# Feed-forward part of a transformer layer on one core: batch 1's rows loaded first, gathers three tiles ahead, and VectorE's closing work in another order

## The reference

```python
h = _layernorm(x) * (1 + ca) + sa
x = x + ga * attn(h, wq, wkv_a, wkv_b, wo)
h = _layernorm(x) * (1 + cb) + sb
# ffn(h): the expert is w2(gelu(h @ g + gb) * (h @ w1 + b1)) + b2
aff = sigmoid(h @ wa); p, i = top_k(aff, 2); p = p / sum(p)
ffn = h + sum over the 2 shared experts + sum over the 2 chosen experts of p * expert(h)
x = x + gb * ffn
```

## Time and profile before

| | us |
|---|---|
| median of 3 runs | 1361.8 |
| lowest and highest | 1360.68, 1362.64 |
| the profiled execution's own time | 1362.64 |
| its span, first to last instruction | 1360.8 |
| TensorE busy | 1321.8 (97%) |
| VectorE busy | 850.3 (62%) |
| ScalarE busy | 687.1 (50%) |
| POOL busy | 384.3 (28%) |

### The profile page before, as it was taken

The page is one execution under the profiler, slowest core; times in us unless marked ns, Lnnn a source line. Parts: engine busy times, 40 slices in busy tenths (PEclk is TensorE's granted clock), DMA queues, the critical chain, the costliest instruction groups (busy, mean ns, idle before and its releaser), DMA issues. The chain is left out here.

```text
span 1360.8 us, 22755 instructions
## 1 busy us (share of the span) xinstructions
PE 1321.8 (97%) x6836; PEld 1102.7 (81%) x6836; DVE 850.3 (62%) x1753; ACT 687.1 (50%) x1615; POOL 384.3 (28%) x353
## 2 busy tenths in 40 slices
PE   6899999999999999999999999997999999999997
PEld 3667777888888888888888888886887888888886
DVE  5788755666666666666666777666666444344568
ACT  3334427666666666666666776663312323232232
POOL 0336465000013092030550302800032232323164
PEclk9999999999999999999999999999999999999999
DMA  9999989967677769696687899793646999894375
GB/s 290 382 343 375 369 299 319 341 223 237 205 276 272 237 231 327 206 341 207 226 301 268 289 316 329 278 354 146 246 156 244 336 347 363 289 368 172 128 235 171
DMA packets 160057, 375.57 MB, mean 276 GB/s; under 512 B 23164, under 2 KB 80576, under 8 KB 147696
## 3 DMA queue, kind: packets, MB, share of 16 engines
q1 hardware_dynamic: 144416, 314.32, 66.0%
q0 software_dynamic: 15568, 60.32, 12.5%
HBM read 245.84 MB, written 128.22 MB: 275 GB/s over the span
## 5 line engine op out<-in xcount | busy, mean ns | idle before, releaser
L1193 ACT ACTIVATE a_pr<-a_pr,a_stat 128x128 f32<-128x128 f32 (+3 forms) x256 | 141.9, 555 | 71.4 <-DVE a_stat L1272 71.4
L1212 ACT ACTIVATE a_pT<-x_banks 128x512 fp32r<-128x512 f32 (+1 forms) x192 | 87.1, 531 | 75.6 <-PE x_banks L1415 75.6
L1199 ACT ACTIVATE a_pr<-a_pr,a_stat 128x128 f32<-128x128 f32 (+3 forms) x256 | 122.3, 550 | 0.5 <-DVE a_stat L1277 0.5
L1399 PE MATMUL x_banks<-a_pT,a_cv 128*128 128x512 f32 (+1 forms) x576 | 120.5, 354 | 0.3 <-issue 0.3
L1399 PEld LDWEIGHTS x_banks<-a_pT,a_cv 128*128 128x128 f32 x576 | 103.4, 188 | 21.2 <-issue 0.7
L1272 DVE CUSTOM_DVE_ANT_0 a_pr<-a_psS,f_mask 128x256 f32<-128x256 f32 (+2 forms) x192 | 101.2, 555 | 23.7 <-PE a_psS L1387 23.3
L1300 DVE TENSOR_TENSOR a_pT<-x_banks,a_pT 128x512 fp32r<-128x512 f32 (+1 forms) x192 | 103.4, 594 | 12.6 <-ACT a_pT L1212 12.6
L101 PE MATMUL x_banks<-a_hT,a_wqk 128*128 (+1 forms) x256 | 99.9, 390 | 1.0 <-DVEq L1259 1.0
L102 PE MATMUL x_banks<-a_hT,a_wqk 128*128 (+1 forms) x256 | 99.7, 390 | 0.0
L103 PE MATMUL x_banks<-a_hT,a_wqk 128*128 (+1 forms) x256 | 99.6, 389 | 0.0
L1288 DVE SCALAR_TENSOR_TENSOR a_qT<-x_banks,a_qT 128x512 fp32r<-128x512 f32 x64 | 44.3, 692 | 85.6 <-ACT a_qT L1203 85.6
(11 more groups left out here) (378 smaller groups left out, 3611.9 us busy)
## 6 DMA issues: line engine op xcount, KB each, us to landing
w1s_d<-a_ws SPq DMA_DIRECT2D x72, 512.0 KB, 3.5
a_wqk<-wqk_d SPq DMA_DIRECT2D x64, 512.0 KB, 5.0
a_mh<-mhl_d SPq DMA_DIRECT2D x32, 1024.0 KB, 5.9
s_ring<-w1s_d SPq DMA_DIRECT2D x16, 2048.0 KB, 10.0
w2s_d<-a_ws SPq DMA_DIRECT2D x72, 256.0 KB, 3.9
qpe_d<-p_qs SPq DMA_DIRECT2D x16, 1024.0 KB, 5.1
a_rw<-in_L_ffn_rw SPq DMA_DIRECT2D x128, 128.0 KB, 3.5
a_qpe<-qpe_d SPq DMA_DIRECT2D x64, 256.0 KB, 2.7
```

The costliest lines, as they stand in the source:

```text
L1193: nc.scalar.activation(pr[i], pr[i], ACT.Exp, bias=nmax[:, i:i + 1], scale=-1.0, accum_out=rsum[:, i:i + 1]).then_inc(ex, 1)
L1199: nc.scalar.activation(pr[i], pr[i], ACT.Copy, scale=rinv[:, i:i + 1]).then_inc(nr, 1)
L1212: nc.scalar.activation(pT[:, u, 0, dst], src, ACT.Copy).then_inc(p_hi, 1)
L1399: last = nc.tensor.matmul(two_of(bank)[:, :, (2 - k) * P:2 * P], cv[:, j, cs], pT[:, :, ps, o:o + k * P], start=m == 0, stop=m == len(part ...
```

## The change

Three edits.

1. In SP's list `rows(1, 1)` stands ahead of the three small transfers on `wa_in`.
2. `AHEAD` is 3: gathers are issued when the tile three before has landed. (SP's wait for `turns[AHEAD - 1]` is written `turns[1]`, the same as before.)
3. VectorE's and ScalarE's lists at the end are rewritten. Tile 2 is taken after slice 2 of batch 3 rather than slice 3. In batch 2 ScalarE scales two to three tiles more ahead of the gelus. VectorE does `weighted` of tiles 9 to 13 ahead of time; tiles 12 and 13 and 15 no longer use `finish` but three new functions: `gated` (the sum times the gate row), `based` (plus the residual) and `joined` (the product from `final` times the gate row into `ys`, and that added). So of these tiles the multiplication and the residual do not need the products.

```diff
-        AHEAD = 2
+        AHEAD = 3
-        tiles_m = {LAST: [[], [0], [1], [2, 3, 4, 5, 6, 7, 8]], 2: [[9], [10], [11], []]}
+        tiles_m = [[], [0], [1, 2], [3, 4, 5, 6, 7, 8]]
...
+                rows(1, 1)
                 sp.dma_start(waf[:, :, :], K.ins["L0_ffn_wa"].rearrange("(c p) e -> p c e", p=P)).then_inc(wa_in, 16)
                 sp.dma_start(bst[0:SH], K.ins["L0_ffn_sgb"]).then_inc(wa_in, 16)
                 sp.dma_start(bst[SH:2 * SH], K.ins["L0_ffn_sb1"]).then_inc(wa_in, 16)
-                rows(1, 1)
                 rows(2, 0)
...
-                for m in range(NU):
+                scaled(9)
+                scaled(10)
+                for m, i in enumerate((11, 13, 14, 15)):
                     gelu(2, m)
+                    scaled(i)
                     y_high(2, m)
-                    if m < NU - 1:
-                        scaled(9 + m)
-                for i in range(12, 16):
-                    scaled(i)
+                    if m == 0:
+                        scaled(12)
...
+                def gated(i):
+                    dve.wait_ge(cch, done[0])
+                    tt_(at[:, i % NA], at[:, i % NA], gb4[:, turns[i] // TB], ALU.mult).then_inc(cch, 1)
+                    done[0] += 1
+                def based(i):
+                    b, t = turns[i] // TB, turns[i] % TB
+                    dve.wait_ge(cch, done[0])
+                    dve.wait_ge(s_in[b], 16)
+                    tt_(at[:, i % NA], at[:, i % NA], total[b][:, t], ALU.add).then_inc(cch, 1)
+                    done[0] += 1
+                def joined(i):
+                    n, b, t = done[0], turns[i] // TB, turns[i] % TB
+                    dve.wait_ge(sh_o, place_of[b] * TB + t + 1)
+                    if i == NT - 1:
+                        dve.wait_ge(o_ok, i - 1)
+                    tt_(ys[:, i % 2], final[b][t], gb4[:, b], ALU.mult).then_inc(cch, 1)
+                    dve.wait_ge(cch, n + 1)
+                    tt_(at[:, i % NA], at[:, i % NA], ys[:, i % 2], ALU.add).then_inc(o_ok, 1)
+                    done[0] = n + 1
...
-                for m in range(NU):
-                    times(2, m)
-                    y_low(2, m)
-                    if m < NU - 1:
-                        whole(9 + m)
-                for i in (12, 13, 14):
-                    weighted(i)
-                finish(12)
-                finish(13)
+                weighted(9)
+                weighted(10)
+                times(2, 0)
+                weighted(11)
+                y_low(2, 0)
+                finish(9)
+                weighted(12)
+                times(2, 1)
+                gated(12)
+                y_low(2, 1)
+                finish(10)
+                weighted(13)
+                times(2, 2)
+                based(12)
+                y_low(2, 2)
+                finish(11)
+                gated(13)
+                times(2, 3)
+                based(13)
+                y_low(2, 3)
+                weighted(14)
                 weighted(15)
+                gated(15)
+                joined(12)
+                based(15)
+                joined(13)
                 finish(14)
-                finish(15)
+                joined(15)
```

More of the change, by code:

```diff
@@ L1742, in _ @@
                     sp.wait_ge(y_out[v], 16 * ((NBLK - v + 1) // 2))
-                sp.wait_ge(r_in[turns[AHEAD - 1]], 32)
+                sp.wait_ge(r_in[turns[1]], 32)
                 sp.dma_start(total[2][:, :, :], K.base_d[2].rearrange("t p n -> p t n")).then_inc(s_in[2], 16)
@@ L1904, in _ @@
                     y_high(LAST, m)
-                    for i in tiles_m[LAST][m]:
+                    for i in tiles_m[m]:
                         scaled(i)
-                for m in range(NU):
+                scaled(9)
+                scaled(10)
+                for m, i in enumerate((11, 13, 14, 15)):
                     gelu(2, m)
+                    scaled(i)
                     y_high(2, m)
-                    if m < NU - 1:
-                        scaled(9 + m)
-                for i in range(12, 16):
-                    scaled(i)
+                    if m == 0:
+                        scaled(12)
             @block.vector
```

## The result

The changed kernel takes 1358.34 us (median of 12 runs, 1357.48 to 1359.76) against 1360.95 for the kernel before on the same chip (12 runs, 1358.53 to 1363.16): ratio 0.9979, 95% interval 0.9970 to 0.9988, a gain of 2.6 us. I forecast 1359.7 and a gain of 2.1. The profiled execution of the changed kernel took 1359.19 us, its span 1357.4.

The account below looks back on a forecast made before the run. TensorE is busy 97% of the span, so gains lie in the first transfer, the gathers' pace and VectorE's list. Front 0.4 plus end 1.7 gave 2.1 us off the 1361.8 median: 1359.7, range 1356.9 to 1362.9 for 8 in 10.

Parts of the forecast that it names:

- likeliest case: Whole kernel: gain of 1 to 3.2 us, around 1359.7, own range 1358.6 to 1360.8; chance 0.42.
- front's gain: Start of the feed-forward part: issuing batch 1's rows earlier gains 0.4 us, between 1.1 gained and 1.2 lost.
- W: Front: time at which the small transfers on `wa_in` are complete, put at 948.5, ends 945 and 950.
- VectorE's side: Front: VectorE, waiting for the small transfers, can start the second `times` at W + 14.7, 963.2; TensorE allows 962.8.
- TensorE's transposes 0.8 to 1.1 us sooner: Front, sign of edit 1: batch 1's transposes start that much sooner after the barrier.
- L2035's counterpart 3 to 4 us later: Front, sign of edit 1: VectorE's operation on the router's weights, behind `wa_in`, starts that much later.
- The gathers: POOL from tile 4 on: three in flight give 2.75 us a tile instead of 3.50, plus 1.1 for stalls.
- Rival C: Gathers: third tile in flight brings no pace, DMA engines set it; 3.9 later at the end, 1365.3; chance 0.12.
- The lists: End: 13 operations instead of 16 behind the last `y_low`, 9.3 us; VectorE ends at S + 20.1, 1.7 us gained.
- S: End: time at which ScalarE can scale tile 13, put at 1336.5, ends 1332.7 and 1342.1.
- A: End: gathers come sooner, S at 1334.7 or before, tail's floor gives 3.5; gain 3.9 to 4.6, 1357.6; chance 0.26.
- B: Gain cancels: front loses up to 1.2 through `wa_in`, or S lies near 1338.2; 1361.5; chance 0.20.

Follow-up runs that it names:

- small_last: The changed kernel with the three small transfers behind both batches' rows: 1363.11 us, ratio 1.0012 to the kernel before.
- changed_again: The changed kernel measured once more, unaltered, beside other kernels on one chip: 1358.34 us, ratio 0.9983 to the kernel before.
- tail_only: The changed kernel with batch 1's rows back behind the small transfers (edits 2 and 3 without 1): 1359.35 us, ratio 0.9993 to the kernel before.
- tail_again: Edits 2 and 3 without edit 1, the same kernel timed in another job: 1357.1 us, ratio 0.9978 to the kernel before.
- lists_only: The changed kernel with AHEAD = 2 and the small transfers first (edit 3 alone): 1363.85 us, ratio 1.0030 to the kernel before.
- no_lists: The kernel before with edits 1 and 2, ScalarE's and VectorE's lists as before: 1359.32 us, ratio 0.9988.
- ahead3_only: The kernel before with AHEAD = 3 alone (edit 2), lists as before: 1358.37 us, ratio 0.9986.
- small_on_pool: The changed kernel with the three small transfers issued by POOL at the block's start: 1362.04 us, ratio 1.0006 to the kernel before.

## Why the prediction held, step by step

The forecast was 1359.7, the result 1358.34, inside the range of 1356.9 to 1362.9 and 0.3 below the likeliest case's own edge of 1358.6. Of the 1.4 us by which the time came below the forecast, 0.85 are the baseline (1361.8 from three runs, 1360.95 from twelve) and 0.5 the gain. The range is no strong test: the kernel before, at 1360.95, lies in it too. What can be tested are the parts. The mechanism at the end held, with one size off; the front's gain did not show. That a front taken 0.4 too well and an end taken 0.3 to 1.4 too low partly cancel is luck.

**W and VectorE's side.** Predicted: W 6.6 us after SP's first issue, `times` at W + 14.7. Measured: 5.7, and 963.77 - 949.43 = 14.3. `wa_in` does hold VectorE, as predicted. "TensorE's transposes 0.8 to 1.1 us sooner" and "L2035's counterpart 3 to 4 us later" came as about 1.3 sooner (950.03 - 943.87 = 6.2 after the part's start, before 7.5) and 2.8 later (5.86 after it against 3.05). Both lie just outside what I had named, and the second `times`, 1.5 us sooner in the profiled pair, does too. Off by 0.9 was W, since the rows landed in 5.4 us and not in 6.44. I had carried over a duration, and it goes with the place in SP's list: 6.3 to 6.5 us in the five traces with the small transfers ahead of the rows, 5.2 to 5.5 in the nine with the rows first, in small_last too, where the second 1 MB follows right behind. Why is open.

**The front's gain, 0.4.** This step is not borne out. Timed alone edit 1 has 1.0007 (0.9998, 1.0016), which leaves room for a gain of 0.3 us at most; with edit 2 beside it it has 0.9988 against 0.9986 without it, and with edits 2 and 3 0.9979 and 0.9983 against 0.9993 and 0.9978. But what I subtracted from was unsound: the 21.39 us of before hold 6.8 us at the lower clock, and I wrote that the clock didn't matter since VectorE's side has no product in it. That is so after the edit; before it TensorE's side decided. By the traces, what edit 1 does is to trade a front of 19.1 to 21.4 for one of 19.9.

**The gathers.** Predicted 2.75 a tile and 1.1 of stalls over nine tiles, 2.87 together; measured 2.83. Tile 15 was issued at 1334.36, ahead of the 1337 that I had named. Rival C rested on a DMA share of 0.95 with two tiles in flight; over 1306 to 1322 us the share rose from 0.85 to 0.93, and the pace came all the same: a share near 1 did not show a bound. The term that I mis-sized is the way from a tile's first issue to ScalarE's use: 6.0 taken, 1334.27 - 1329.33 = 4.94 measured, below my lowest row (5.6). That put `scaled(13)` at 41.0 us after the first gather, not at 42.6, and so at 1334.27 and not at 1336 to 1337, and the last `y_low` at 1345.46 and not at 1347 to 1348. Single gathers of the changed kernel took this long from issue to landing, over 1303 to 1340 us:

```profile
DMA to landing us min/median/max: 3.6/4.7/7.0
```

With the second gather 1.26 us behind the first, a tile takes 4.9 us at the least and 6.0 at the median; my 6.0 was the median, and tile 13 had the least, in changed_again too (40.43 - 35.50 = 4.9).

**The lists.** Last `y_low` to VectorE's end: 9.3 predicted, 9.38 measured. `scaled(13)` to VectorE's end: 20.1 predicted, 1354.84 - 1334.27 = 20.6 measured. S sooner by 1.6 and 0.5 more behind it give 1.1 more than my 1.7, 2.8: the end won 2.7 us in the profiled pair, 3.1 in changed_again and 2.0 in tail_only and tail_again. TensorE waited 0.5 us in batch 2 (0.22 + 0.25), where I had allowed 2.

**Rivals.** A (floor, 1357.6) wants `scaled(13)` at 1334.7 or before, which is 40.8 after the first gather of the kernel before; it came at 41.0 and, in changed_again, at 40.4, where the end won 3.1 of A's 3.5. So the result lies between forecast and A, as the time does. B is half right: edit 1 cancels itself, as far as the times can tell. C's mechanism is real, shown by lists_only with TensorE's wait of 3.06 us, and three tiles in flight avert it; its premise, that the third tile brings no pace, was wrong.

**What stays open.** How much edit 3 gives once three tiles are in flight: 0.4 to 0.5 us at the end by the traces (64.63 to 64.16, 65.33 to 64.9), and in the medians 1.0 won (no_lists to changed, on two chips) or anything from 1.0 lost to 1.3 won (ahead3_only to tail_only and to tail_again), under the 2 us by which one kernel differs from itself between jobs. Whether edit 1 costs anything: 1.0007 allows from 0.3 us won to 2.2 lost. And why the end is up to 1 us shorter where edits 1 and 3 are together (64.16, 63.75) than with 3 alone (64.93, 64.90): I have no row for it.

## What to carry to other kernels

Where one edit is safe only with another, time them apart and together: the new lists alone lose 4 us, and the deeper prefetch that makes them safe is most of the gain by itself. When a large transfer is moved ahead of small ones, look who waits for the small ones and what independent work stands behind that wait. Here the reordering alone gave no gain that the times could tell; moving 3.2 us of VectorE's sums into the wait took 2.0 us more off the front (the time's ratio went to 0.9974, an interval that meets the changed kernel's). And before a stretch of one profiled execution is taken as the baseline of a term, read the granted clock in it.

## What I had not expected of the hardware

- The same front (same instructions, same order) took 19.1, 20.0 and 21.4 us, with 3.4 or 6.8 us of it at TensorE's lower level; the kernel before ran from 1357.8 to 1363.4 us within one job.
- 36 KB in three small transfers are in ScalarE's use 2.0 us after the part's first VectorE instruction when they are issued first (before), 5.6 behind 1 MB (changed), 8.5 from POOL's queue beside 4 MB of SP's (small_on_pool), and 9.95 behind twice 1 MB on SP's (small_last).
- The same 1 MB of rows landed 6.3 to 6.5 us after its issue with the small transfers ahead of it, and 5.2 to 5.5 us as SP's first.
- An idle time of 3.06 us of TensorE in lists_only was followed by a stretch at a granted clock of 0.62 (4 us), which costs 1.5 us, half as much again on top of the wait.
